# Deformable convolution stage: eight-unit rings, four transpose banks, and evacuations and half-products issued later

## The reference

```
om   = conv3x3(groupnorm(x), w_off) + b_off          # 27 channels
off, mask = om[:18], sigmoid(om[18:])
for tap t of 9, output pixel p:
    py, px = base(t, p) + off(t, p)                  # a fractional position
    sampled[:, t, p] = mask(t, p) * sum over 4 corners (weight * value at the corner)
out[o, p] = sum over c, t of w_dcn[o, c, t] * sampled[c, t, p] + b_dcn[o]
x = x + out
```

## Time and profile before

| | |
|---|---|
| median of the runs | 5587.88 us (5573.19 to 5591.83) |
| span of the profiled execution | 5878.0 us |
| mean granted TensorE clock in it | 0.884 |
| deformable stage in it | from the first gather at 3813.1 us to about 5875 us |
| instructions of the stage | 1152 gathers, 1152 `pa`, 3 x 1152 VectorE operations, 576 copies, 2304 transposes, 2304 matmuls |

### The profile page before, as it was taken

How to read it: one execution, slowest core, us unless ns; L and a number is a source line. 1 busy time by engine, 2 the same in 40 slices (tenths; PEclk the granted TensorE clock), 3 DMA queues, 4 the chain that set the end, 5 groups by cost and what they waited for, 6 DMA issues and landing times. The chain is left out here.

```text
span 5878.0 us, 77391 instructions
## 1 busy us (share of the span) xinstructions
PE 4391.9 (75%) x18884; PEld 1919.9 (33%) x18884; DVE 3868.0 (66%) x6758; ACT 2372.6 (40%) x4441; POOL 3241.3 (55%) x1968
## 2 busy tenths in 40 slices
PE   2888888888888888886366795776766777776767
PEld 0222222222222222221366642233333333333333
DVE  5888888888888888885000082276766766776767
ACT  0455555555555555554000053243333333343333
POOL 0567666676666766667011111166666666666665
PEclk8899999999999999998688897888888888898889
DMA  4011111111111111110999978698888888888887
GB/s 152 27 51 52 48 38 48 44 47 46 44 49 51 52 49 37 48 37 26 218 192 186 177 293 227 176 331 312 308 303 295 311 312 300 316 327 309 309 309 289
DMA packets 503233, 991.54 MB, mean 169 GB/s; under 512 B 53281, under 2 KB 291489, under 8 KB 486353
## 3 DMA queue, kind: packets, MB, share of 16 engines
q0 software_dynamic: 165888, 604.05, 28.1%
q1 hardware_dynamic: 336976, 383.47, 25.9%
HBM read 831.01 MB, written 104.96 MB: 159 GB/s over the span
## 5 line engine op out<-in xcount | busy, mean ns | idle before, releaser
L1354 POOL DMA_INDIRECT gat<-gather_table,idc x1152 | 1332.4, 1157 | 781.1 <-DVE sm L1436 409.1
L402 POOL TENSOR_TENSOR psum<-psum,pr 128x1024 f32<-128x1024 f32 x576 | 1495.7, 2615 | 409.2 <-ACT pr L470 400.0
L514 DVE TENSOR_REDUCE nmx<-mring 128x1 f32<-128x512 f32 x2048 | 1304.8, 681 | 443.4 <-PE mring L645 435.5
L470 ACT ACTIVATE pr<-ering 128x512 f32<-128x512 f32 x2048 | 1150.5, 598 | 1003.7 <-PE ering L665 993.3
L1470 PE MATMUL pac<-smt,wds 128*128 128x512 f32 x2304 | 1170.8, 655 | 219.0 <-ACT smt L1369 163.4
L645 PE MATMUL mring<-ks,qs 96*128 96x512 f16 x2048 | 869.4, 425 | 249.2 <-DVE nmx L514 241.6
L665 PE MATMUL ering<-qs,ks 98*128 98x512 f16 x2048 | 836.6, 417 | 157.9 <-DMA qs<-mlo 118.5
L1422 DVE SCALAR_TENSOR_TENSOR pbb<-gat,wtc,pa 128x256 f32<-128x256 f32 x1152 | 509.5, 480 | 569.3 <-ACT pa L1379 374.3
L1369 ACT COPY smt<-ptr 128x512 f32<-128x512 f32 x576 | 335.4, 582 | 1229.3 <-PE ptr L1482 755.3
L1470 PEld LDWEIGHTS pac<-smt,wds 128*128 128x128 f32 x2304 | 462.4, 212 | 736.9 <-issue 553.8
L1482 PE MATMUL ptr<-cst,sm 128*128 128x128 f32 x2304 | 378.2, 293 | 388.4 <-DVE sm L1436 334.7
(11 more groups left out here) (131 smaller groups left out, 2730.9 us busy)
## 6 DMA issues: line engine op xcount, KB each, us to landing
toep<-toe SPq DMA_DIRECT2D x64, 1280.0 KB, 17.6
gather_table<-pix SPq DMA_DIRECT2D x64, 512.0 KB, 8.4
va<-v_pixel_major SPq DMA_DIRECT2D x40, 512.0 KB, 7.5
gat<-gather_table,idc POOLq DMA_INDIRECT x1152
xs<-xa SPq DMA_DIRECT2D x16, 1024.0 KB, 4.8
xin<-xa SPq DMA_DIRECT2D x16, 1024.0 KB, 4.8
qs<-qkh SPq DMA_DIRECT2D x256, 64.0 KB, 2.0
ks<-qkh SPq DMA_DIRECT2D x256, 64.0 KB, 2.0
```

The source lines that it names most:

```text
L402: gp.tensor_tensor(psum[:, g, h, :], pr[:, 0, h, :] if m == 1 else psum[:, g, h, :], pr[:, m % 2, h, :], ALU.add).then_inc(s_pa, 1)
L470: act.activation(pr[:, m % 2, h, c * 512:(c + 1) * 512], ering[n % 2][:, :], ACT.Exp).then_inc(s_e, 1)
L514: dve.tensor_reduce(nmx[:, g, n // CH, n % CH:n % CH + 1], mring[n % 2][:, :], AX.X, ALU.max, negate=True).then_inc(s_mf, 1)
L1354: gp.indirect_dma_start(gat[:, r, :, :].rearrange("p q c -> p (q c)"), None, tab, bass.IndirectOffsetOnAxis(ap=idc[:, e, u:u + 1], axis=0) ...
```

## The change

In the deformable stage alone:

- `pa`, `pbb`, `pb` and `sm` become rings of 8 units (`NP`), and the transposes get 4 PSUM banks (`RPT`).
- ScalarE evacuates pair q - 2 (`LAG`) after `pa` of pair q, not q - 1, and carries this on over the boundary between groups and between iterations.
- TensorE issues half a product (one `o`, four matmuls) after the transposes of each pair, four pairs late (`PLAG`), over the boundaries too, and not a whole one after every second pair.
- VectorE no longer waits for the gathers itself, waits once per pair for both `pa`, and does `finish` after pair 9 (`FIN`), not 3.
- For ScalarE and TensorE the first iteration stands outside the loop, and what is left over is drained behind it.

```diff
-            NP = 4
+            NP = 8
+            NPAIR = NP // 2
+            RPT = 4
+            LAG = 2
+            FIN = 9
+            PLAG = 4
...
-            ptr = [pb(st, f"ptr6_{n}", [P, 2, KC, P]) for n in range(3)]
+            ptr = [pb(st, f"ptr6_{n}", [P, 2, KC, P]) for n in range(RPT)]
...
-                                if u % 2 and u >= 3:
-                                    evac(e, u // 2 - 1)
-                            evac(e, PAIRS6 - 1)
+                                if u % 2:
+                                    q = u // 2 - LAG
+                                    if q >= 0:
+                                        evac(i, e, q)
+                                    elif e:
+                                        evac(i, 0, PAIRS6 + q)
+                                    elif not first:
+                                        evac(i - 1, 1, PAIRS6 + q)
+
+                    turn(0, True)
+                    with act.Fori(1, IT) as i:
+                        turn(i, False)
+                    for q in range(PAIRS6 - LAG, PAIRS6):
+                        evac(IT - 1, 1, q)
...
-                                    dve.wait_ge(s_g[u % RING],
-                                                i * (2 * PER) + (e * PER + (u // RING + 1) * 16))
-                                    dve.wait_ge(s_p0, i * (2 * UNITS) + (n + 1))
+                                    if s == 0:
+                                        dve.wait_ge(s_p0, i * (2 * UNITS) + (n + 2))
...
-                                if q == 3 and e:
+                                if q == FIN and e:
                                     finish(i, 0)
-                                elif q == 3 and not (isinstance(i, int) and i == 0):
+                                elif q == FIN and not (isinstance(i, int) and i == 0):
                                     finish(i - 1, 1)
...
+                    def product(i, e, n):
+
+                        tap, o = n // KC, n % KC
+                        if o == 0:
+                            pe.wait_ge(s_te, i * (2 * PAIRS6) + (e * PAIRS6 + 2 * tap + 2 + RPT))
                             if tap == 0:
-                                pe.wait_ge(s_fin, (i * 2 + e + 1) * KC)
...
+                                pe.wait_ge(s_fin, i * (2 * KC) + (e + 1) * KC)
+                        for k in range(KC):
+                            mm = pe.matmul(pac[e][o][:, :], wds[:, k, tap, o * P:(o + 1) * P],
+                                           smt[:, tap % 3, k, :], start=tap == 0 and k == 0,
+                                           stop=tap == TAPS - 1 and k == KC - 1)
+                        if o == KC - 1:
                             mm.then_inc(s_mm, 1)
...
-                                if q >= 2 and q % 2 == 0:
-                                    product(e, q // 2 - 1)
-                            product(e, TAPS - 1)
+                                if q >= PLAG:
+                                    product(i, e, q - PLAG)
+                                elif e:
+                                    product(i, 0, PAIRS6 + q - PLAG)
+                                elif not first:
+                                    product(i - 1, 1, PAIRS6 + q - PLAG)
+
+                    turn(0, True)
+                    with pe.Fori(1, IT) as i:
+                        turn(i, False)
+                    for q in range(PAIRS6 - PLAG, PAIRS6):
+                        product(IT - 1, 1, q)
```

More of the change, by code:

```diff
@@ L1359, in _ @@
                 def _(act):
[L1360 to L1370, removed]
+                    act.sem_inc(s_te, RPT)
@@ new lines, in evac @@
+                    def evac(i, e, q):
+                        n = e * PAIRS6 + q
+                        tap, half = q // 2, q % 2
+                        act.wait_ge(s_tr, i * (2 * PAIRS6) + (n + 1 + NPAIR))
+                        if half == 0:
+                            act.wait_ge(s_mm, i * (2 * TAPS) + (e * TAPS + tap + 1))
+                        act.copy(smt[:, tap % 3, :, 256 * half:256 * half + 256].rearrange(
+                            "p k (t n) -> p t k n", t=2), ptr[n % RPT][:, :, :, :]).then_inc(s_te, 1)
@@ L1372, in _, with turn @@
+                    def turn(i, first):
                         for e in range(2):
-                            act.wait_ge(s_idr, i * 2 + e + 1)
+                            act.wait_ge(s_idr, i * 2 + (e + 1))
                             for u in range(UNITS):
                                 n = e * UNITS + u
-                                act.wait_ge(s_g[u % RING], (i * 2 + e) * (UNITS // RING) * 16 + (u // RING + 1) * 16)
-                                act.wait_ge(s_sm, i * (2 * UNITS) + n + 1 + RING - NP)
+                                act.wait_ge(s_g[u % RING], i * (2 * PER) + (e * PER + (u // RING + 1) * 16))
+                                act.wait_ge(s_sm, i * (2 * UNITS) + (n + 1 + RING - NP))
@@ L1459, in _, with turn @@
                     pe.wait_ge(s_w, 32)
-                    pe.sem_inc(s_tr, 2)
+                    pe.sem_inc(s_tr, NPAIR)
                     pe.sem_inc(s_mm, 3)
-                    with pe.Fori(0, IT) as i:
-                        def product(e, tap):
-                            pe.wait_ge(s_te, i * (2 * PAIRS6) + e * PAIRS6 + 2 * tap + 2 + 3)
+                    def product(i, e, n):
+                        tap, o = n // KC, n % KC
+                        if o == 0:
+                            pe.wait_ge(s_te, i * (2 * PAIRS6) + (e * PAIRS6 + 2 * tap + 2 + RPT))
                             if tap == 0:
-                                pe.wait_ge(s_fin, (i * 2 + e + 1) * KC)
[L1468 to L1472, removed]
+                                pe.wait_ge(s_fin, i * (2 * KC) + (e + 1) * KC)
[4 more added lines that the diff above has]
+                        if o == KC - 1:
                             mm.then_inc(s_mm, 1)
+                    def turn(i, first):
                         for e in range(2):
@@ L1477, in _ @@
                                 n = e * PAIRS6 + q
-                                pe.wait_ge(s_sm, i * (2 * UNITS) + 2 * n + 2 + RING)
-                                pe.wait_ge(s_te, i * (2 * PAIRS6) + n + 1)
+                                pe.wait_ge(s_sm, i * (2 * UNITS) + (2 * n + 2 + RING))
+                                pe.wait_ge(s_te, i * (2 * PAIRS6) + (n + 1))
                                 for s in range(2):
                                     for k in range(KC):
-                                        mm = pe.transpose(ptr[n % 3][:, s, k, :],
+                                        mm = pe.transpose(ptr[n % RPT][:, s, k, :],
                                                           sm[:, (2 * n + s) % NP, k * P:(k + 1) * P], ident)
                                 mm.then_inc(s_tr, 1)
-                                if q >= 2 and q % 2 == 0:
-                                    product(e, q // 2 - 1)
-                            product(e, TAPS - 1)
+                                if q >= PLAG:
[9 more added lines that the diff above has]
+                        product(IT - 1, 1, q)
 def kernel(x, **w):
```

## The result

The changed kernel takes **5660.11 us** (median; 5651.66 to 5678.16), the kernel before beside it 5588.02 us (5573.19 to 5591.83): a ratio of **1.0145**, 95% interval 1.0123 to 1.0167. It is 72 us slower. The forecast was 89 us faster, and 5660 lies above the range.

A forecast was written before the change was run, and what follows sets the result against it. GpSimd's gather issuing was taken as the bound: a timed gather phase of 1754 us would fall to 1665 (1635 plus 30 of remaining waits), 89 us less, so 5587.9 becomes 5499 us; range 5425 to 5580.

The forecast's parts named there:

- GpSimd's own 1635 us: Gather issue in the deformable stage: 1332.4 us busy plus 302.3 us idle that no one released, held fixed.
- "Nothing" for `finish`: Moving `finish` from q=3 to q=9: same 64 instructions, nobody waits sooner than a group later, so priced at no time.
- rival A: Long gathers come from completion hangs; without them the bytes bind at 1592 us, 162 us less, 5426; chance 0.18.
- Boundary: Between groups: VectorE idle of 16 x 3.21 + 15 x 4.66 = 121 us removed, of which 106 us go.
- the 3.17 inside the first pair: VectorE stall in us inside a new iteration's first pair, with nothing to release it; expected to stay.
- The timed execution: Profile 290 us longer than timed runs, laid to TensorE completion hangs; timed gather phase about 1754 us, 119 of it waits.
- Rings and banks: Rings of eight, four banks: no instruction added, 4.7 us more cover for `sm` ahead of the transposes.
- Waits: VectorE's fewer waits, but both `pa` awaited per pair: cost between 0 and 265 us, taken as 0.
- Clock (C): TensorE's gaps lower its mean clock to 0.75: 1889 us needed, 135 us slower, 5723; chance 0.08.
- DMA engines (B): DMA engines bind the stage already: 20 us left to gain, 5568, or none, 5588; chance 0.16.
- the sign set for B: ScalarE's `pa` beginning to wait for gathers for over 200 us would show the DMA engines binding and the forecast wrong.
- D: TensorE's completion hangs are in timed runs too, so deeper rings cover 4.7 us of each: 256 us, 5332; chance 0.04.

The follow-up runs named there:

- second profile of before: The kernel before, profiled again with no edit: span 5564.9 us, 5566.67 us timed, no remote wait.
- the gap: VectorE waits after each pair for its own last `sm`: 5447.69 us (0.9774) in the changed kernel, 5628.23 us (1.0099) in the kernel before.

## Why the prediction was wrong, step by step

**The step that failed** is the claim that GpSimd's own 1635 us are a constant, and with it the word "Nothing" for `finish`. The sum had 1332.4 busy and 302.3 without a releaser. After it is 1465.2 + 357.6 less the 67.9 ahead of the first gather, 1754.9 us; the second profile of before has 1327.9 + 277.3 = 1605.2 by the same working (its first "issue" is 69.3). That is 150 us more of what the sum held fixed. The waits for `sm` fell by 56, and 150 - 56 = 94 us is what the gather phase grew by. The mean of 1157 ns beside a median of 940 was the sign, and I priced only its going away (rival A), not its growth. The prediction asked what the moved instructions cost and who waits for them; it did not ask what they let through by standing where they stood.

**The size of it, from runs.** Old order and `finish` at 9: +93 us. New order and `finish` at 9: +72 beside its own kernel before (1.0145). Everything else in the change, with `finish` held at 9, is 1.0145 against 1.0164, 11 us with intervals that overlap; with the lockout gone, by a memset in both, it is 62 to 69 us, and with the gap in both 180. So the boundary, the evacuations and the halves are worth what a sum without the lockout would have said (rival A came out at 5426, the memset version at 5442, with the bytes as the bound, as A had it), and in the kernel as it stands the lockout takes it back. A's reason was wrong all the same: it put the long gathers down to the hangs, and the second profile has the same mean, 1153 ns, with no remote wait.

**Boundary.** The mechanism was right inside an iteration, and not where a new one begins. Inside an iteration the first `pbb` of a group was idle 2.58 us ahead on average in the second profile of before and 0.10 after. Entering a new iteration it was 4.04 and is 4.02. In 14 of the 15 both `pa` had ended 3.5 to 4.8 us before VectorE began, so the 4.66 did not go: nothing in the profile releases the stall that I had put on the evacuation ("issue" in the row above). It stands where VectorE's loop begins anew; the one entry that has none (0.12 us) is the first, from the code ahead of the loop. The sum had also taken one boundary of each kind, 3.21 and 4.66, for all 31; their means are 2.58 and 4.04. What went there is the 3.17 inside the first pair, which I had kept: it is 2.99 on average in the second profile of before, and 0 after. And the idle of VectorE came back elsewhere: ahead of pairs 6 and 7 it is 3.13 and 2.42 us on average in the iteration's first group, ahead of pair 14 3.47, where gathers had been locked out.

**The timed execution.** That 290 us belong to the profiled execution alone was right: 1754 us were taken for the gather phase of a timed run and 119 for its waits; the second profile has 1724.9 and 119.7. That they belong to being profiled was not: the second profile, like all later ones, has none. What caused them in that one execution stays open.

**Rings and banks:** nothing, as held for the case that GpSimd is the bound; shown with the gap, where the bytes bind, and not tried without it. **Waits:** taken at 0, measured as no loss, with a gain of 35 us where `finish` is at 5. **Clock (C):** it was 0.92 in the stage, 0.94 before; no collapse. **DMA engines (B):** their share is 0.91 after, so they don't bind there; but the sign set for B, `pa` waiting for gathers over 200 us, appeared (850.1) for another reason. They bind at 400 GB/s and share 1.00 in the versions without lockout, against the 358 GB/s per core of the Trainium skill (DMA: Bandwidth & Descriptors, Where 436 GB/s comes from), which the page gets by halving a stack's rate between two cores; here one core runs. **D** fell with the second profile.

**What beats both kernels:** the changed kernel with the memset (0.9760), or with the gap and rings of four (0.9754). `finish` at pair 9 does no harm there.

## What to carry to other kernels

Where GpSimd issues gathers beside a VectorE that runs instructions with two SBUF inputs back to back, the issue can be held over many of them (80 of 1152 gathers here, for up to 10 us); look at the mean against the median of the gathers, and at whether the long ones end at a fixed distance behind a VectorE instruction. A change that moves the one instruction of another kind to another place in the stream can cost more than it brings, and a cheap instruction of another kind after every few gives it back. Before a sum is made, compare the profile's span with the timed runs, and if they differ, don't lean on its waits.

## What the runs showed of the hardware that I had not expected

- A gather's issue of 0.94 us was held up to 11.2 us by VectorE instructions of 0.48 us each that start 0.40 apart. Of the 837 that meet one in the profile after, 535 pass in under 1.0 us, 216 end 0.81 us after the end of one, and 80 are held over many.
- A memset of 128x32 (85 ns in the mean) after six such instructions lets it through, at 0.04 us a pair for VectorE. The longest gather is then 1.27 us. A wait of VectorE for its own last instruction does the same.
- Moving the two PSUM-reading instructions of each group by six pairs, in a stream otherwise unchanged, cost 93 us of 5581, 1.6%.
- The gathers' packets of 4096 bytes per partition run at 400 GB/s over 1550 us on one core.

What stays open: what decides whether a gather is let in at the end of one instruction or held over many; which of the gather's accesses to SBUF the lock stops (the indices' read, or the writing of descriptors) was not tried, nor was it followed one by one how each block comes from the place of `finish`: the run shows that the place decides, by 93 us, and the excess that it goes with.
